# Biases of the expert and router matmuls put into their weights, and some expert blocks split by VectorE straight from PSUM

## The reference

```python
x = x + tanh(g_xattn) * attention(layernorm(x), ctx, ctx, mask, Wq, Wk, Wv, Wo)
x = x + tanh(g_ffn) * ffn(layernorm(x))

def ffn(x):                                  # rows of 128
    probs = softmax(x @ Wg + bg)
    w, idx = top_k(probs, 2);  w = w / sum(w)
    comb = sum(one_hot(idx) * w)
    h = relu(einsum('nd,edh->enh', x, W1) + b1[:, None, :])
    y = einsum('enh,ehd->end', h, W2) + b2[:, None, :]
    return einsum('end,ne->nd', y, comb)
```

## Time and profile before

| what | value |
| --- | --- |
| median of 3 runs | 1075.51 us (1074.73 to 1077.64) |
| the profiled execution | 1077.04 us |
| its span | 1075.3 us |
| TensorE busy | 1018.8 us, 95% |
| ScalarE busy | 941.9 us, 88% |
| VectorE busy | 855.8 us, 80% |
| GpSimd busy | 815.0 us, 76% |
| mean granted TensorE clock | 0.991 of full |

### The profile page before, as it was taken

How to read it: one execution, slowest core, us unless ns; L and a number is a source line. 1 busy time by engine, 2 the same in 40 slices (tenths; PEclk the granted TensorE clock), 3 DMA queues, 4 the chain that set the end, 5 groups by cost and what they waited for, 6 DMA issues and landing times.

```text
span 1075.3 us, 36365 instructions
## 1 busy us (share of the span) xinstructions
PE 1018.8 (95%) x13797; PEld 754.7 (70%) x13797; DVE 855.8 (80%) x1739; ACT 941.9 (88%) x1809; POOL 815.0 (76%) x815
## 2 busy tenths in 40 slices
PE   6878899999999999999999999999999999999986
PEld 4456667777776777777677777777777777777754
DVE  2587687897988789798878978887897888878667
ACT  3899889889898988989898898989889898989775
POOL 3586668778787877887787788778778887889943
PEclk9899899999999999999999999999999999999999
DMA  9122121212112121211212121122212211112100
GB/s 225 30 53 72 49 59 44 58 46 61 46 48 61 44 61 44 62 47 46 56 51 58 43 63 49 44 56 54 58 44 61 51 31 46 46 41 52 30 3 21
DMA packets 123163, 56.90 MB, mean 53 GB/s; under 512 B 26584, under 2 KB 122864, under 8 KB 122992
## 3 DMA queue, kind: packets, MB, share of 16 engines
q1 hardware_dynamic: 122992, 54.59, 20.3%
HBM read 16.80 MB, written 4.19 MB: 20 GB/s over the span
## 4 chain that ended last, share of the span: by engine, by line
PE 59%; POOL 11%; DVE 10%; ACT 10%; issue 9%; DMA 1%; POOLq 0%; ACTq 0%; SPq 0%; DVEq 0%
PE bank L44 18%; PE bank L46 17%; PE bank L45 17%; PE bank L308 3%; POOL rstd L866 3%; POOL hidL L885 3%; PE bank L263 2%; POOL ptL L922 2%; ACT bank L521 2%; ACT qH L465 2%; DVE comb L850 1%; DVE above L826 1%; ACT vH L560 1%; ACT pt L580 1%; POOL prob L928 1%
## 5 line engine op out<-in xcount | busy, mean ns | idle before, releaser
L885 POOL TENSOR_TENSOR hidL<-hid,hidH 128x512 f16<-128x512 f32 x242 | 278.4, 1165 | 18.0 <-ACT hidH L495 17.8
L922 POOL TENSOR_TENSOR ptL<-pt,ptH 128x512 f16<-128x512 f32 x128 | 149.4, 1167 | 130.1 <-ACT pt L580 130.1
L665 DVE TENSOR_TENSOR qL<-bank,qH 128x512 f16<-128x512 f32 x224 | 153.4, 685 | 61.5 <-ACT qH L465 58.2
L485 ACT ACTIVATE hid<-bank,b1col 128x512 f32<-128x512 f32 x256 | 188.9, 738 | 8.9 <-PE bank L46 8.7
L495 ACT ACTIVATE hidH<-bank,b1col 128x512 f16<-128x512 f32 x256 | 191.5, 748 | 0.0
L465 ACT ACTIVATE qH<-bank 128x512 f16<-128x512 f32 x256 | 158.6, 622 | 36.8 <-PE bank L46 35.8
L44 PE MATMUL bank<-w2H,hidH 128*128 128x128 f16 x1024 | 178.1, 219 | 9.8 <-DVE hidL L776 4.9
L46 PE MATMUL bank<-w2H,hidL 128*128 128x128 f16 x1024 | 178.1, 219 | 0.0
L45 PE MATMUL bank<-w2L,hidH 128*128 128x128 f16 x1024 | 178.1, 219 | 0.0
L917 POOL TENSOR_TENSOR x<-x,y_scaled 128x512 f32<-128x512 f32 x114 | 145.9, 1280 | 13.8 <-DVE x L734 13.8
L928 POOL TENSOR_TENSOR prob<-prob,row_inv 128x512 f32<-128x512 f32 x128 | 133.5, 1043 | 15.3 <-DVE row_inv L770 15.3
(11 more groups left out here) (144 smaller groups left out, 3597.0 us busy)
## 6 DMA issues: line engine op xcount, KB each, us to landing
vdH<-vH SPq DMA_DIRECT2D x256, 64.0 KB, 2.1
vdL<-vL SPq DMA_DIRECT2D x256, 64.0 KB, 2.1
x_raw<-in_x SPq DMA_DIRECT2D x16, 256.0 KB, 2.9
ctx_raw<-in_ctx SPq DMA_DIRECT2D x16, 256.0 KB, 3.2
mask_raw<-in_fside_Bx1xSxS SPq DMA_DIRECT2D x32, 128.0 KB, 2.8
out_x<-x SPq DMA_DIRECT2D x16, 256.0 KB, 2.4
qH<-in_L_xattn_Wq SPq DMA_DIRECT2D x1, 512.0 KB, 5.3
qH<-in_L_xattn_Wk SPq DMA_DIRECT2D x1, 512.0 KB, 7.1
```

The lines of the kernel that those rows point to most:

```text
L485: act.activation(hid[:, k % NR, :], bk("hid", g, e, c)[:, :], ACT.Relu, bias=b1col[:, e, c:c + 1]).then_inc(s_relu[c], 1)
L665: dve.tensor_tensor(qL[at], bk("Q", g, h)[:, :].rearrange("p (b q) -> p b q", b=GB), qH[at], ALU.subtract).then_inc(s_q_low[h % 2], 1)
L885: pool.tensor_tensor(hidL[:, m % 2, c, :], hid[:, k % NR, :], hidH[:, m % 2, c, :], ALU.subtract).then_inc(s_hid_low[c], 1)
L922: pool.tensor_tensor(ptL[:, b % 2, :], pt[:, b % 2, :], ptH[:, b % 2, :], ALU.subtract).then_inc(s_pt_low, 1)
```

## The change

The layernormed rows sum to zero. The kernel adds SHIFT = 1 to each element of the transposed normed rows (`x2T`, a constant in the copy on ScalarE and an add in VectorE's subtraction), so each row sums to 128. A number added to a whole column of a weight matrix then adds 128 times that number to each output. W1 becomes W1 + (b1 - column sums of W1) / 128: the column sums take off what the shift added, b1 / 128 brings the bias. This is worked out once: TensorE makes, in steps 0 and 1 behind the second hidden half's place, 16 f32 matmuls of 256 columns into four banks (for each expert b1 spread over all partitions by a column of the identity, and minus the column sums by a matrix of -1), and VectorE adds each bank divided by 128 into the raw W1 at the end of steps 1 and 2. The two ScalarE copies of W1 in steps 2 and 3 wait for that. For the router only the column sums of Wg are taken off, in the row `bgrow`, ahead of the loop; its logits keep their add. `b1col` is gone. b1 is loaded as 8 rows into the place of `x2hat`, and bg is loaded earlier.

With no bias left, VectorE can make the low half in one instruction from PSUM: max(bank, 0) - hidH. This is done (`direct(m, c)`) for c = 1 where m % 8 is 1, 4 or 7, and for both halves from block 114 on. Where it is done, ScalarE doesn't write `hid` and GpSimd doesn't subtract. GpSimd makes all sums of `y_scaled` again, those of the last blocks too. The buffers of `hid` are counted over the blocks that still use them, and the bank of such a block is free when VectorE has read it.

```diff
+SHIFT = 1.0
+AFTER_WEIGHTS = H // 4 + 2 * (C // CL) + 1
...
+        def direct(m, c):
+            return m >= TAIL or (c == 1 and m % E % 3 == 1)
+
+        hid_staged = [(m, c) for m in range(GROUPS * E) for c in range(HC) if not direct(m, c)]
+        relu_at, hid_low_at = {}, {}
+        for c in range(HC):
+            by_pool = by_dve = 0
+            for m in range(GROUPS * E):
+                if direct(m, c):
+                    by_dve += 1
+                    hid_low_at[m, c] = (s_hid_direct[c], by_dve)
+                else:
+                    by_pool += 1
+                    relu_at[m, c] = (s_relu[c], by_pool)
+                    hid_low_at[m, c] = (s_hid_low[c], by_pool)
...
-                return [(s_relu[c], g * E + e + 1), (s_hid_high[c], g * E + e + 1)]
+                m = g * E + e
+                return [hid_low_at[m, c]] if direct(m, c) else [relu_at[m, c], (s_hid_high[c], m + 1)]
...
-            for freed in take_bank("b1T", 0):
+            for freed in take_bank("bias row", 0):
                 pe.wait_ge(*freed)
-            pe.wait_ge(s_load["b1"], 16)
-            pe.transpose(bk("b1T", 0)[:, 0:E * HC], b1_raw, ident[0:E * HC, 0:E * HC]).then_inc(s_wpe, 1)
+            pe.wait_ge(s_load["Wg"], 16)
+            pe.wait_ge(s_minus_one, 1)
...
+                if s in (0, 1):
+                    for n in (2 * s, 2 * s + 1):
+                        for freed in take_bank("shift W1", n):
+                            pe.wait_ge(*freed)
+                        if n == 0:
+                            pe.wait_ge(s_load["b1"], 16)
+                        if n % 2 == 0:
+                            pe.wait_ge(s_load["W1" + "ab"[s]], 16)
+                        for k in range(2):
+                            cols = slice(k * HID, (k + 1) * HID)
+                            pe.matmul(bk("shift W1", n)[:, cols], ident[0:E, 2 * n + k:2 * n + k + 1].to_broadcast([E, P]),
+                                      b1_raw, start=True, stop=False, skip_group_check=True)
+                            last = pe.matmul(bk("shift W1", n)[:, cols], minus_one[:, :],
+                                             w1_raw[s][:, (n % 2) * N + k * HID:(n % 2) * N + (k + 1) * HID],
+                                             start=False, stop=True, skip_group_check=True)
+                        last.then_inc(s_wpe, 1)
...
-                k = m * HC + c
-                act.wait_ge(s_hid, k + 1)
-                if k >= NR:
-                    act.wait_ge(*hid_lowered((k - NR) // HC, (k - NR) % HC))
-                else:
-                    act.wait_ge(*q_low_at[STAGED[k - NR]])
-                act.activation(hid[:, k % NR, :], bk("hid", g, e, c)[:, :], ACT.Relu,
-                               bias=b1col[:, e, c:c + 1]).then_inc(s_relu[c], 1)
+                k = hid_staged.index((m, c))
+                act.wait_ge(s_hid, m * HC + c + 1)
...
+                act.activation(hidH[:, m % 2, c, :], bk("hid", g, e, c)[:, :], ACT.Relu).then_inc(s_hid_high[c], 1)
...
-            act.wait_ge(s_wpe, H // 4 + 5)
-            act.activation(b1col[:, :, :].rearrange("p e c -> p (e c)"), bk("b1T", 0)[:, 0:E * HC],
-                           ACT.Copy, scale=WS).then_inc(s_b1col, 1)
...
-                if within(eg, GROUPS):
+                if within(eg, GROUPS) and not direct(eg * E + ei, 0):
                     hidden_relu(eg, ei, 0)
...
-                    hidden_relu(eg, ei, 1)
+                    if not direct(eg * E + ei, 1):
+                        hidden_relu(eg, ei, 1)
...
+                    act.wait_ge(s_w1_shifted, 2 * (s - 1))
...
+            def hidden_low(m, c):
+                dve.wait_ge(s_hid_high[c], m + 1)
+                dve.scalar_tensor_tensor(hidL[:, m % 2, c, :], bk("hid", m // E, m % E, c)[:, :], 0.0, hidH[:, m % 2, c, :],
+                                         ALU.max, ALU.subtract).then_inc(s_hid_direct[c], 1)
...
+            dve.wait_ge(s_wpe, AFTER_WEIGHTS)
+            dve.wait_ge(s_load["bg"], 16)
+            dve.tensor_tensor(bgrow[:, :], bk("bias row", 0)[:, 0:E], bgrow[:, :], ALU.add).then_inc(s_bias_row, 1)
...
+                    dve.wait_ge(s_x2T_high, pg)
+                    dve.scalar_tensor_tensor(x2tL[:, (pg - 1) % 2, :], bk("x2T", pg - 1)[:, :], SHIFT,
+                                             x2tH[:, (pg - 1) % 2, :], ALU.add, ALU.subtract).then_inc(s_x2T_low, 1)
...
-                m = s - 3 - FFN_LAG
-                if within(m, GROUPS * E) and m >= TAIL:
-                    dve.wait_ge(s_scaled, m + 1)
-                    dve.wait_ge(*(y_added(m - 1) if m % E else (s_ln[1]["rows"], m // E + 1)))
-                    if m % E == BIAS_AT:
-                        dve.wait_ge(s_b2_add, m // E + 1)
-                    acc = x2[:, m // E % NX2]
-                    dve.tensor_tensor(acc, acc, y_scaled[:, m % 2], ALU.add).then_inc(s_y_tail, 1)
...
                     dve.reciprocal(row_inv[:, b % NPB, :], row_sum[:, b % NPB, :]).then_inc(s_inv, 1)
-                if within(eg, GROUPS) and eg * E + ei >= TAIL:
-                    m = eg * E + ei
-                    k = m * HC + 1
-                    dve.wait_ge(s_relu[1], m + 1)
-                    dve.wait_ge(s_hid_high[1], m + 1)
-                    dve.tensor_tensor(hidL[:, m % 2, 1, :], hid[:, k % NR, :], hidH[:, m % 2, 1, :],
-                                      ALU.subtract).then_inc(s_hid_tail, 1)
+                if within(eg, GROUPS):
+                    for c in range(HC):
+                        if direct(eg * E + ei, c):
+                            hidden_low(eg * E + ei, c)
                 if within(s, B):
...
+                if s in (1, 2):
+                    for n in (2 * s - 2, 2 * s - 1):
+                        raw = w1_raw[s - 1][:, n % 2 * N:(n % 2 + 1) * N]
+                        dve.wait_ge(s_wpe, AFTER_WEIGHTS + n + 1)
+                        dve.scalar_tensor_tensor(raw, bk("shift W1", n)[:, :], 1.0 / P, raw, ALU.mult,
+                                                 ALU.add).then_inc(s_w1_shifted, 1)
...
-                if within(m, TAIL):
+                if within(m, GROUPS * E) and not direct(m, 1):
                     hidden_low(m, 1)
                 m = s - 3 - FFN_LAG
-                if within(m, TAIL):
+                if within(m, GROUPS * E):
                     pool.wait_ge(s_scaled, m + 1)
...
-                if within(m, GROUPS * E):
+                if within(m, GROUPS * E) and not direct(m, 0):
...
-            load("b1", b1_raw, b1.rearrange("e (c p) -> (e c) p", p=P))
+            load("bg", bgrow[:, :], bg.unsqueeze(0).to_broadcast([P, E]))
+            load("b1", b1_raw, b1)
```

More of the change, by code:

```diff
@@ L166, in flamingo_block @@
             sem(n) for n in ("v_low", "max", "shift", "sum", "inverse", "o_low", "residual"))
-        s_scaled, s_b2_add, s_y_tail, s_hid_tail = (sem(n) for n in ("y_scaled", "b2_add", "y_add_tail", "hid_low_tail"))
+        s_scaled, s_b2_add = (sem(n) for n in ("y_scaled", "b2_add"))
+        s_hid_direct = [sem(f"hid_low_direct{c}") for c in range(HC)]
         s_marked, s_mask_in = sem("score_banks_marked"), sem("mask_in_bank")
@@ L242, in evicted @@
                 return [(s_wdve, at[0] + 1)]
-            counted = {"b1T": s_b1col, "xT": s_xT_low, "ctxT": s_ctxT_low, "x2T": s_x2T_low, "logitT": s_logitT_out,
+            counted = {"bias row": s_bias_row, "shift W1": s_w1_shifted, "xT": s_xT_low, "ctxT": s_ctxT_low, "x2T": s_x2T_low, "logitT": s_logitT_out,
                        "logit": s_logit_in, "pickedT": s_pickT_low, "b2 out": s_b2_add}
@@ L384, in _ @@
                     last.then_inc(s_wpe, 1)
-            for freed in take_bank("b1T", 0):
+            for freed in take_bank("bias row", 0):
                 pe.wait_ge(*freed)
-            pe.wait_ge(s_load["b1"], 16)
-            pe.transpose(bk("b1T", 0)[:, 0:E * HC], b1_raw, ident[0:E * HC, 0:E * HC]).then_inc(s_wpe, 1)
+            pe.wait_ge(s_load["Wg"], 16)
+            pe.wait_ge(s_minus_one, 1)
+            pe.matmul(bk("bias row", 0)[:, 0:E], minus_one[:, :], wg_raw, start=True, stop=True).then_inc(s_wpe, 1)
             transposes("xT", 0, xhat, (s_ln[0]["rows"], 1), s_xT)
@@ L478, in hidden_relu @@
                 m = g * E + e
-                k = m * HC + c
-                act.wait_ge(s_hid, k + 1)
-                if k >= NR:
-                    act.wait_ge(*hid_lowered((k - NR) // HC, (k - NR) % HC))
-                else:
-                    act.wait_ge(*q_low_at[STAGED[k - NR]])
-                act.activation(hid[:, k % NR, :], bk("hid", g, e, c)[:, :], ACT.Relu,
-                               bias=b1col[:, e, c:c + 1]).then_inc(s_relu[c], 1)
+                k = hid_staged.index((m, c))
+                act.wait_ge(s_hid, m * HC + c + 1)
+                act.wait_ge(*(hid_low_at[hid_staged[k - NR]] if k >= NR else q_low_at[STAGED[-1]]))
+                act.activation(hid[:, k % NR, :], bk("hid", g, e, c)[:, :], ACT.Relu).then_inc(s_relu[c], 1)
```

(9 more changed lines are left out.)

36 lines of the change are left out of this document (15 added, 21 removed).

## The result

The changed kernel takes 1096.67 us (median of 4 runs, 1093.29 to 1099.33) against 1075.16 us (4 runs): 1.0194 times as long, 95% interval 1.0153 to 1.0234. Its profiled run is its fastest, 1093.29 us with a span of 1091.6 us, so the traces stand 16.3 us apart and the medians 21.5 us.

A forecast was written before the change was run, and what follows sets the result against it. TensorE was taken to set the pace from step 16, ScalarE with GpSimd before it. The terms 8 + 0.3 + 23.8 + 8.4 + 5.6 - 2.6 - 4 = 39.5 us led to 1115 us, range 1086 to 1140.

The forecast's parts named there:

- Where the new block stands: VectorE's in-order queue: the direct block waits for ScalarE's last `hidH` and holds the shift, `otL` and the router's chain.
- What would show it: Signs: VectorE idle some 1.9 us for `hidH`, TensorE waiting 1 to 2 us for `otL` or the residual, `comb` near 0.24 us.
- Step i = 1: Second step of each group of eight: late `otL` and residual cost 1.7 us a group, 23.8 us in all (20 to 36).
- the 0.83 us of `comb`: Router's chain in i = 1: time taken off because `comb` runs later, with one GpSimd `hidL` less there.
- Steps i = 4 and 7: Late VectorE blocks delay TensorE's banks in the next step: 0.6 and 0.4 us a group, 8.4 and 5.6 us in all.
- The start: Steps 0 and 1: 16 f32 matmuls for W1 ahead of the query blocks, 8 us (4 to 9), plus 0.3 for the bias row.
- The fourth bank's wait: W1 matmuls in steps 0 and 1: TensorE waits until VectorE has added the reused first bank, 1.8 us more.
- The end: From expert block 114 on: TensorE's waits for VectorE's `hidL` behind ScalarE's four blocks shrink, 4 us gained (0 to 5).
- Relief wins: Rival: ScalarE, relieved of three blocks a group, runs ahead, so VectorE does not stand in i = 1; 1070 us, chance 0.10.
- A part of the stand is hidden: Rival: ScalarE comes 0.9 us earlier in i = 1, nothing shows in 4 and 7; 0.8 us a group, 1088 us, chance 0.16.
- The clock falls: Rival: new holes in TensorE's work halve its clock for 6.8 us in every second group; 24 us, 1139 us, chance 0.12.

## Why the prediction was right, and where its sizes were off

The time, 1096.67 us, lies in the range 1086 to 1140, slower as forecast, and 18 us below the forecast of 1115. The mechanism was right in each of its two places, and four terms were mis-sized. Between the two traces 39.5 us were forecast and 16.3 measured: the middle cost 22.1 us less than its terms (13.1 for 35.2), the end gave 3.1 us more, and the start cost 2.0 us more. Part of the agreement is luck. The traces alone would give 1091.8 us, just at the lower bound of my sum (1092); the 5 us by which the medians stand further apart have no term in the prediction.

**Where the new block stands: shown.** The behaviour named under "What would show it" is in the rows: VectorE idle 1.53 us for `hidH` (1.85 worked out), `comb` at 0.24 us, TensorE waiting for `otL` and the residual. Moving the block alone gave the middle 13.8 us back; leaving it out of i = 1 alone gave 15.0.

**Step i = 1: 1.7 us a group forecast, 1.1 measured** (i = 1 and 2 in the table of step lengths); over 14 groups 23.8 us and 15, below my lower end of 20. The wait, the chain and the 0.83 us of `comb` were right. The term was too large by what the chain wins otherwise, as the rows show when they are counted from the gate's exponential (522.52 before, 537.80 after):

- The new block starts at 5.69 us where I had 5.98. I took ScalarE's blocks at the durations of the trace and priced the removal of their bias operand at nothing, without naming it at all.
- `otL` ends at 7.58 us where I had 8.05. I took 0.69 us for each of three blocks; VectorE starts such blocks every 0.61 us.
- The residual starts at 9.98 us, against 8.91 before: 1.07 us later and not 1.7. Between `otL` and `comb` the chain won 0.2 us more, for which I had nothing.

The kernel with the bias column tells which of these counted. There the new block starts at 5.95 us, as I had it, and i = 1 and 2 still cost 1.07 us a group. What makes up for it is a small block of the router's chain ahead of `comb`. In the kernel before, in the changed kernel and with the column:

```profile
529.03 0.65 DVE L845 TENSOR_TENSOR picked<-picked,picked_inv 128x32 f32<-128x32 f32 x1
```

```profile
545.74 0.47 DVE L867 SCALAR_TENSOR_TENSOR picked<-rank,expo 128x32 f32<-128x32 f32 x1
546.67 0.19 DVE L874 TENSOR_TENSOR picked<-picked,picked_inv 128x32 f32<-128x32 f32 x1
```

```profile
548.77 0.69 DVE L701 SCALAR_TENSOR_TENSOR hidL<-bank,hidH 128x512 f16<-128x512 f32 x1 [1.79 <-ACT hidH L523]
551.02 0.19 DVE L870 SCALAR_TENSOR_TENSOR picked<-rank,expo 128x32 f32<-128x32 f32 x1
551.67 0.19 DVE L877 TENSOR_TENSOR picked<-picked,picked_inv 128x32 f32<-128x32 f32 x1
```

Run later, beside an idle GpSimd, the second `picked` wins 0.46 us like `comb`. In the changed kernel the chain comes 0.3 us earlier, and its first `picked` loses that again (0.47 us for 0.20) beside GpSimd's sum, which ends at 546.16. So in i = 1 the missing column is not what made my term too large; the block spacing and the small blocks of the chain are.

**Steps i = 4 and 7: 8.4 and 5.6 us forecast, nothing measured.** The hold is there, 1.53 us of idle, but slack covers it. VectorE and TensorE of the changed kernel in i = 4 and the next step:

```profile
567.37 0.69 DVE L698 SCALAR_TENSOR_TENSOR hidL<-bank,hidH 128x512 f16<-128x512 f32 x1 [1.53 <-ACT hidH L521]
568.58 0.68 DVE L812 TENSOR_TENSOR otL<-bank,otH 128x512 f16<-128x512 f32 x1
570.63 0.66 DVE L739 TENSOR_TENSOR y_scaled<-bank,comb 128x512 f32<-128x512 f32 x1
...
571.34 0.22 PE L46 MATMUL bank<-ptH,vdH 128*128 128x64 f16 x1
```

`y_scaled` ends at 571.29 and TensorE takes the bank at 571.34. Here the missing column did count, and the experiment shows it: with the column back, TensorE waits 0.3 us for `y_scaled` in 12 groups, and the steps lengthen by 0.26 us in i = 5 and 0.28 in i = 7, of the 0.6 and 0.4 that I had. The 0.2 us from the blocks' spacing is about the rest. Over the whole middle the column accounts for 8.6 of the 22.1 us by which I was off.

**The start: 8.3 us forecast, 10.3 in the traces.** I read 32 records of the earlier trace rows as 32 matmuls. The source has 16 there; each f32 matmul leaves two records, so one of 128 columns takes 0.43 us and not 0.22. One of 256 columns takes 0.63, not 0.44, so the 16 take 10 us and not 7. The fourth bank's wait was named rightly and is 0.76 us, not 1.8, since TensorE came later. With these two figures my own sum gives 10 + 0.8 - 0.6 = 10.2 us; the two errors partly made up for each other. The clock is not needed for it: up to step 16 the changed kernel's trace has some 10 us at half clock and that of the kernel before some 17. That the loss stays until step 16 was right.

**The end: 4 us forecast, 7.1 measured.** I took only the part of TensorE's waits for VectorE's `hidL` in the earlier trace rows. From 920 us on these fall from 4.9 to 0.5 us, and the waits for GpSimd's `hidL`, 2.2 us, go too.

**The rivals.** "Relief wins" is refuted by VectorE's idle time of 1.53 us in i = 1, by the kernel before without the column, and by the equal times with and without direct blocks in the middle. "A part of the stand is hidden" (1088 us) was nearer than my own sum: nothing shows in i = 4 and 7, as it says, and its group cost of 0.8 us is near the measured 0.9. But ScalarE came 0.3 us earlier and not 0.9. "The clock falls" did not come in the middle (1.00 from 300 to 400 us); at the start the clock did fall.

**Open.** The four runs of the changed kernel lie at 1093.3, 1094.1, 1099.2 and 1099.3 us, with mean clocks of 0.995, 0.993, 0.988 and 0.986. The longer the run, the lower its clock, and this may be the difference of some 5 us between the traces' 16.3 and the medians' 21.5. Only the first of them has a trace, so where the clock was low in the others is not known. The length of the half-clock stretch at the f32 matmuls alone does not explain it: the kernel with the moved block has 6.8 us there and the changed kernel 3.4, and they reach step 16 at 148.12 and 148.43 us.

## What to carry to other kernels

Before an engine is relieved, read what the pacing engine waits for: here 9.5 us in 740. Nothing that took load off the other engines gave more than 2 us in the middle, while a swap of two blocks in the queue of the engine that is waited for gave 9.9 us. A new block in an in-order queue costs by its wait and by what is queued behind it; put it behind everything that someone is waiting for. An operand that goes has a price too: look at the same instruction with and without it. And what an earlier result is worth depends on the whole chain behind it: in i = 1 ScalarE's 0.3 us were lost again in a small block of the router's chain.

## What the runs showed of the hardware

**A bias column costs time on ScalarE.** A 128x512 relu from PSUM takes 0.72 to 0.74 us with a column of zeros and 0.63 to 0.64 us without, in kernels that otherwise do the same work. In the kernel before and its run without the column it is 0.75 to 0.76 and 0.64 to 0.66 us. The Trainium skill, ScalarE: Activation LUTs, section What ACT_TABLE_LOAD costs, gives some 93 ns for each such column operand; the runs here agree with 0.10 us. The prediction did not draw on it for the operand that the change takes away.

**f32 matmuls.** Each is two records, and 256 columns follow each other at 0.63 us, whether 8 or 128 rows are in use (57.79, 58.41 and 59.04 above).

**The clock fell while TensorE was at work.** TensorE ran these matmuls from 54.45 on with a single wait of 0.76 us, and at 59.4 us the granted clock went from 1.00 to 0.50, from 2.4 to 1.2 GHz. The changed kernel first, then the one with the moved block:

```profile
46.00:59.40 13.40, 12.63 (x87) 6.88 (x87) 6.69 (x12) 4.72 (x10) 4.42 (x4) 1.00 0.21 42
59.40:62.80 3.40, 3.40 (x9) 1.41 (x8) 0.00 (x0) 0.38 (x1) 0.00 (x0) 0.50 0.00 0
```

```profile
57.60:64.40 6.80, 6.80 (x15) 2.80 (x16) 0.27 (x1) 1.49 (x3) 0.00 (x0) 0.50 0.05 10
64.40:75.00 10.60, 8.15 (x123) 5.55 (x121) 10.05 (x16) 10.60 (x21) 8.66 (x7) 1.00 0.21 40
```

The other engines did little in that time. The fall of the earlier trace rows followed a wait of TensorE of 2.62 us; this one follows a stretch busy with f32 matmuls. It belongs to them: in all five traces that have them in steps 0 and 1, the mean granted clock from 50 to 75 us is 0.86 to 0.93, and in the eight others it is 1.00. With the same matmuls spread over steps 2 to 9, the clock stays at 1.00 from 46 to 110 us. What about these matmuls brings the clock down, their kind or that many of them follow each other, was not tested.
